# Shared remainder tiles in the last group of a graph-attention kernel, with a reordered lead-in and split borders

## The chip, the cores and the metric

One core of a Trainium2 chip runs the whole program. The metric is device time in microseconds (us). Five engines work side by side: TensorE (PE, with its weight loads as PEld), VectorE (DVE), ScalarE (ACT), GpSimd (POOL) and SyncE (SP, which here only issues DMAs). The kernel before takes 1327.33 us, the median of 3 runs from 1325.82 to 1328.85.

## The reference

A graph of 6250 nodes with 96 features and 106250 edges (50000 random ones in both directions, and a loop at every node). Each edge has a row node (`src`) and a column node (`dst`).

```python
q = (x[src] @ qW).reshape(e, 4, 24)
k = (x[dst] @ kW).reshape(e, 4, 24)
v = (x[dst] @ vW).reshape(e, 4, 24)
exp_s = exp(clip(einsum('ehd,ehd->eh', q, k), -10, 10))
norms = segment_sum(exp_s, src)[src]
w = exp_s / (norms + 1e-8)
res = segment_sum(w[:, :, None] * v, src).reshape(6250, 96)
y = x + (x + res)
out = (y - mean(y)) / sqrt(var(y) + 1e-5)      # over the 96 features
```

## The kernel before

The 6250 nodes are 49 blocks of 128. The kernel projects all nodes once: q stays in SBUF (`qt`), k and v go to a table in DRAM (`kv_table`, 192 numbers a row). The edges must be ordered by the block of their row node, because then one tile of 128 edges belongs to one block and a 128x128 one-hot matrix spreads q to the edges and adds the results up. The order is computed on the chip.

**Groups and sort.** The 106250 edges are cut into six groups of 140, 110, 130, 160, 160 and 150 columns of 125 edges. For each group a ranking stage (mostly DVE: `mark`, `tally`, `pair`, `pay`, `count`, `base`, `bounds`, `select`, `table`, `tree`, `own`) finds the place of each edge. Then come sort units (`unit`), one for 10 columns: DVE makes `lhs_1`, `lhs_a` and `lhs_b` (in the memory of `place_m`), ACT makes ten rows of `theta` (in `steps_m`), and PE adds 20 matmuls up in `ps_a` and `ps_b`. A border ends the group: `lower` (ACT copies the sums to `cum_a`, `cum_b`), `differ` (DVE: `dif`), `turn` (PE transposes, ACT copies to `turned`), `choice` (PE picks the tiles) and `pick` (DVE makes `dst_s`, the table rows to gather, and `loc_s`, the place in the block). Pieces of the sort of the next group stand between the batches of the one before.

**Tiles and batches.** A group gives tiles of 128 edges: 85, 110, 125, 155, 155 and 250, in all 880, worked on in 176 batches of five (U = 5). In groups 1 to 5 of the six only full tiles of a block are given out; what a block has left goes to the next group. The last group rounds every block up, so each block may end in a tile that is only partly filled: 250 tiles for 25610 edges (200 full tiles' worth).

**A batch.** POOL issues five indirect DMAs (line 474), each fetching 128 rows of `kv_table` into a slot of `kv`, a ring of R = 8 slots of five tiles. The wait before a batch's first gather is on `s_wv` (batch n-8 was weighed, so its slot is free) and on `s_res` (the results of batch n-6 are made, Y = 6). DVE builds `ohb`, PE transposes it to `ps_t`, ACT copies it to `onehT`, PE spreads q (`ps_q`, line 608), DVE multiplies by k (`prod`, line 1065), reduces and clips, ACT takes the exponential, DVE weighs v (`wv`, line 1074), PE sums (`ps_r`, line 622), DVE adds up in `acc` (line 1047). DVE waits for the gather at line 1065.

**What sets the order.** `plan()` writes a list of pieces and batches once, and each engine follows it, leaving out what it has no part in. In the lead-in the list places `lift` (transposes of x, `copy_xt`) and `project(i)` (seven blocks each) between pieces of the first ranking; `project(i)` of PE and ACT begins with the `lift` of i+1. `plan_last` runs the batches after the last border, 122 to 175, first some straight and then in a loop of eight. The end (`total`, `spread_of`, `root`, `scale_of`) divides, adds 2x and normalizes in four parts.

## Time and profile before

| | |
|---|---|
| median of 3 runs | 1327.33 us |
| profiled execution | 1328.32 us, span 1326.5 us |
| PE busy | 1016.5 us (77%) |
| DVE busy | 1027.9 us (77%) |
| ACT busy | 662.4 us (50%) |
| POOL busy | 935.0 us (70%) |
| gathers | 880, 86.56 MB |
| first gather starts | 97.67 us |
| last gather ends | 1286.34 us |
| mean granted PE clock | 0.716 of 2.4 GHz |

Busy time of an engine leaves out its issuing work. Of POOL above all: between two gathers of a batch the trace shows 0.30 us in which POOL waits for nothing that it shows. So an engine that is 70% busy can be one that never rests. The share says nothing of the stage either: the last stage, 971.5 to 1286.3 us, holds only batches and no sort.

### The profile page before, as it was taken

How to read it: one execution, taken by the hardware profiler on the slowest of the kernel's cores; microseconds unless marked ns; L12 is line 12 of the kernel's file. 1: busy time of each engine (PE TensorE's matmuls, PEld its weight loads, DVE VectorE, ACT ScalarE, POOL GpSimd, SP SyncE). 2: the span in 40 equal slices, each digit the busy share in tenths (PEclk: the TensorE clock that was granted, in tenths of full speed). 3: DMA queues.
4: the chain of work that ended last, by engine and by line, in shares of the span. 5: the costliest groups of instructions: out<-in, count | busy, mean ns of one | idle time of the engine just before them, and what ended most of it. 6: DMA issues, size and time to landing. Idle time of an engine off the chain costs nothing.

```text
span 1326.5 us, 23177 instructions
## 1 busy us (share of the span) xinstructions
PE 1016.5 (77%) x6512; PEld 920.2 (69%) x6513; DVE 1027.9 (77%) x3029; ACT 662.4 (50%) x1469; POOL 935.0 (70%) x912
## 2 busy tenths in 40 slices
PE   7876777688866888767878867877778888888870
PEld 5765776577756787657877656867677777777760
DVE  8889997899799998899977789877655555555557
ACT  5752692269622898224987322878332222222224
POOL 1207777777776777777777777777777777777762
PEclk9996698568975899765989666789765555555555
DMA  6202222222222222222222222222622222222222
GB/s 164 84 0 75 72 67 80 76 67 69 76 78 63 64 73 72 72 73 69 73 69 73 74 78 73 70 72 69 147 80 79 77 79 78 77 80 78 78 65 73
DMA packets 68434, 100.71 MB, mean 76 GB/s; under 512 B 33527, under 2 KB 54004, under 8 KB 68334
## 3 DMA queue, kind: packets, MB, share of 16 engines
q0 software_dynamic: 42240, 86.56, 24.0%
q1 hardware_dynamic: 26094, 12.94, 3.7%
q8 instruction: 47, 0.77, 0.2%
q14 instruction: 53, 0.43, 0.1%
HBM read 92.23 MB, written 7.22 MB: 75 GB/s over the span
## 4 chain that ended last, share of the span: by engine, by line
POOL 29%; DVE 25%; issue 17%; ACT 12%; PE 12%; DVEq 3%; DMA 2%; POOLq 0%; SPq 0%; ACTq 0%
POOL kv L474 28%; ACT steps_m L681 8%; DVE acc L1047 4%; PE ps_r L622 3%; DVE prod L1065 2%; PE ps_q L608 2%; ACT oneh L732 2%; DVE steps_m L806 2%; DMA kv<-kv_table,dst_s 2%; DVE place_m L948 2%; DVEq L391 2%; DVE place_m L952 2%; PE ps_a L594 2%; PE ps_b L594 1%; ACT onehT L726 1%
## 5 line engine op out<-in xcount | busy, mean ns | idle before, releaser
L474 POOL DMA_INDIRECT kv<-kv_table,dst_s x880 | 913.5, 1038 | 319.4 <-issue 313.0
L622 PE MATMUL ps_r<-wv,oneh 128*128 128x100 f32 x1752 | 339.8, 363 | 101.0 <-DVE wv L1074 100.4
L608 PE MATMUL ps_q<-qt,onehT 128*128 x1760 | 332.5, 357 | 97.8 <-ACT onehT L726 90.8
L622 PEld LDWEIGHTS ps_r<-wv,oneh 128*128 128x128 f32 x1752 | 309.2, 269 | 122.1 <-DVE wv L1074 116.2
L608 PEld LDWEIGHTS ps_q<-qt,onehT 128*128 128x128 f32 x1760 | 303.5, 263 | 124.9 <-issue 124.5
L681 ACT ACTIVATE steps_m<-iota_f,pos_t 125x254 f16<-125x254 f32 (+4 forms) x794 | 311.2, 484 | 17.4 <-PE ps_b L594 10.6
L1047 DVE TENSOR_TENSOR acc<-acc,ps_r 128x100 f32 x876 | 222.4, 254 | 58.7 <-issue 24.6
L1065 DVE TENSOR_TENSOR prod<-ps_q,kv 128x480 f32<-128x480 f32 x176 | 115.3, 655 | 175.5 <-DMA kv<-kv_table,dst_s 164.7
L719 ACT ACTIVATE wv<-clipped 128x20 f32<-128x20 f32 x176 | 38.3, 218 | 393.8 <-DVE clipped L1092 393.6
L726 ACT ACTIVATE onehT<-ps_t 128x640 f32<-128x640 bf16 x176 | 123.6, 702 | 180.5 <-PE ps_t L634 168.9
L594 PE MATMUL ps_a<-steps_m,place_m 125*128 125x254 f16 (+4 forms) x794 | 185.2, 283 | 28.6 <-ACT steps_m L681 28.0
L594 PE MATMUL ps_b<-steps_m,place_m 125*128 125x254 f16 (+4 forms) x794 | 183.6, 280 | 0.0
L732 ACT ACTIVATE oneh<-ohb 128x640 f32<-128x640 bf16 x176 | 163.1, 927 | 1.3 <-PE ps_r L622 1.3
L594 PEld LDWEIGHTS ps_a<-steps_m,place_m 125*128 125x128 f16 x794 | 112.3, 141 | 35.2 <-issue 16.0
L1074 DVE TENSOR_TENSOR wv<-kv,wv 128x480 f32<-128x480 f32 x176 | 114.3, 649 | 3.2 <-issue 2.2
L634 PE MATMUL ps_t<-ident_bf,ohb 128*128 128x128 bf16 x880 | 107.0, 271 | 11.7 <-DVE ohb L1055 11.5
L594 PEld LDWEIGHTS ps_b<-steps_m,place_m 125*128 125x128 f16 x794 | 112.8, 142 | 3.3
L1084 DVE TENSOR_REDUCE score<-prod 128x20 f32<-128x480 f32 x176 | 113.7, 646 | 0.2
L634 PEld LDWEIGHTS ps_t<-ident_bf,ohb 128*128 128x128 bf16 x880 | 92.4, 141 | 18.8 <-DVE ohb L1055 17.2
L1055 DVE TENSOR_TENSOR ohb<-iota_t,loc_s 128x640 bf16<-128x640 bf16 x176 | 98.8, 561 | 0.0
L988 DVE TENSOR_TENSOR place_m<-iota_s,pos_p 125x1280 f16<-125x1280 f16 x85 | 69.6, 819 | 8.7 <-PE ps_b L594 8.7
L992 DVE TENSOR_TENSOR place_m<-place_m,pay_a 125x1280 f16<-125x1280 f16 x85 | 69.7, 820 | 1.6
(196 smaller groups left out, 670.1 us busy)
## 6 DMA issues: line engine op xcount, KB each, us to landing
kv<-kv_table,dst_s POOLq DMA_INDIRECT x880
kv_table<-kv SPq DMA_DIRECT2D x7, 672.0 KB, 3.7
acc<-in_x_dram SPq DMA_DIRECT2D x6, 336.0 KB, 8.2
steps_m<-in_x_dram SPq DMA_DIRECT2D x6, 336.0 KB, 6.2
out_dram<-kv SPq DMA_DIRECT2D x6, 336.0 KB
dst_i<-in_dst_dram SPq DMA_DIRECT2D x1, 415.0 KB
src_i<-in_src_dram SPq DMA_DIRECT2D x1, 346.7 KB
acc<-in_x_dram SPq DMA_DIRECT2D x1, 288.0 KB, 4.7
```

Source lines behind the costliest of these rows:

```text
L474: nc.gpsimd.indirect_dma_start(kv[:, nm, u, :], None, kv_dram, bass.IndirectOffsetOnAxis(ap=dst_s[:, n * U + u:n * U + u + 1], axis=0)).th ...
L594: mm = nc.tensor.matmul(ps[:, 0:w], lhs[:, vm, :, j], steps, start=first and j == 0, stop=last and j == SU - 1)
L608: last = nc.tensor.matmul(ps_q[nm % 2][:, u * D:(u + 1) * D], onehT[:, nm % 2, u * P:(u + 1) * P], qt[:, bass.ds(blks[u], 1), :].rearrange ...
L622: last = nc.tensor.matmul(to, oneh[:, nm % 2, u, :], wv[:, nm % 2, u, :], start=True, stop=True)
L634: last = nc.tensor.transpose(ps_t[nm % 2][:, u * P // 2:(u + 1) * P // 2].bitcast(bf16), ohb[:, nm % 4, :, u], ident_bf[:, :])
L681: last = nc.scalar.activation(theta[:, vm, j, 0:w], iota_f[0:EP, 0:w], ACT.Sign, scale=-1.0, bias=pos_t[:, bass.ds(v * SU + j, 1)])
L726: nc.scalar.activation(onehT[:, nm % 2, :], ps_t[nm % 2][:, 0:U * P // 2].bitcast(bf16), ACT.Copy).then_inc(s_oneT, 1)
L732: nc.scalar.activation(oneh[:, nm % 2, :, :], ohb[:, nm % 4, :, :].rearrange("p n u -> p u n"), ACT.Copy).then_inc(s_onf, 1)
L1047: nc.vector.tensor_tensor(at, at, from_ps, ALU.add).then_inc(s_acc, 1)
L1065: nc.vector.tensor_tensor(prod[:, nm % 2, :].rearrange("p (u d) -> p u d", u=U), ps_q[nm % 2][:, 0:U * D].rearrange("p (u d) -> p u d", u= ...
L1074: nc.vector.tensor_tensor(wv[:, nm % 2, :, 0:D].rearrange("p u (h d) -> p u h d", h=HEADS), kv[:, nm, :, D:2 * D].rearrange("p u (h d) -> ...
L1084: nc.vector.tensor_reduce(score[:, nm % 2, :], prod[:, nm % 2, :].rearrange("p (h d) -> p h d", d=DH), axis=AX.X, op=ALU.add).then_inc(s_s ...
```

## The change

1. **Shared remainder tiles** (last group). The 250 tiles are now laid out as 25 pairs of blocks, 50 tiles that stand first, and 200 tiles of whole ones. A pair of blocks shares one gathered tile: the rest of the even block fills it from partition 0 on, that of the odd block from partition 127 down, since the position within a block is flipped for odd blocks (`flip`, an XOR with 127). Where two rests together exceed 128 edges, the odd block gets its own whole tile count instead. Each tile of the pair still has its own block, one-hot and batch, but both read the same slot of `kv`: batches 126 to 135 read the gathered batches 126 to 130, batches 136 to 175 the gathered 131 to 170 (`gathered`, `last_use`). POOL issues 171 batches of five and not 176. DVE, PE and ACT still work through 176.
2. **Gathers of the last group** wait on `s_wv` alone; the earlier ones keep the wait on `s_res`. `plan_last` runs batches straight up to 136 before its loop.
3. **Lead-in.** `project` no longer begins with a `lift`; the plan places both kinds.
4. **Sort units and borders.** PE does the ten matmuls of `ps_a`, then the ten of `ps_b`; the first ten wait for `lhs_a` alone. `lower`, `differ`, `turn` and `pick` signal and wait for each half. `pick` on DVE takes half a first.
5. **Small ones.** Two DVE instructions make `flip` in each group, `bounds` and `pick` of the last group get some more, and the last square root on ACT stands after 9 and not after 12 activations.

```diff
+    PAIRS = -(-NB // 2)
+    MT = 2 * PAIRS
+    GT.append(MT + alone)
...
+    def gathered(n):
+        if not isinstance(n, int) or n >= MB + MT // U:
+            return n - PAIRS // U
+        return n if n < MB else MB + (n - MB) // 2
+
+    def last_use(k):
+        if k < MB:
+            return k
+        return MB + 2 * (k - MB) + 1 if k < MB + PAIRS // U else k + PAIRS // U
...
-        looped = max(m, R)
+        looped = max(m, MB + MT // U + 1)
...
-        project_after = {"mark3": ("lift", 0), f"tally{len(ROUNDS[0]) - 1}": (1,), "base1": (2,),
-                         "table": (3, 4, 5, 6)}
+        between = {"mark3": (("lift", 0), ("lift", 1), ("project", 0)),
+                   f"tally{len(ROUNDS[0]) - 1}": (("lift", 2),), "count": (("project", 1),),
+                   "bounds": (("lift", 3), ("project", 2), ("lift", 4), ("project", 3)),
+                   "table": (("lift", 5), ("project", 4), ("lift", 6), ("project", 5), ("project", 6))}
...
-                for n in range(B0[g], B0[g + 1]):
+                for n in range(B0[g], B0[g + 1] if g < G - 1 else NG):
                     nm = n % R
-                    wait(pool, s_wv, n - R + 1)
-                    wait(pool, s_res, n - Y + 1)
+                    if n >= R:
+                        pool.wait_ge(s_wv, last_use(n - R) + 1)
+                    if Y <= n < MB:
+                        pool.wait_ge(s_res, last_use(n - Y) + 1)
...
-                pe.wait_ge(s_lhs, v + 1)
                 pe.wait_ge(s_theta, v + 1)
-                for j in range(SU):
-                    for ps, lhs in ((ps_a, lhs_a), (ps_b, lhs_b)):
+                for ps, lhs, s_made in ((ps_a, lhs_a, s_lhs_a), (ps_b, lhs_b, s_lhs)):
+                    pe.wait_ge(s_made, v + 1)
+                    for j in range(SU):
...
+                    if last and ps is ps_a:
+                        mm.then_inc(s_half, 1)
...
-                act.wait_ge(s_bin, V0[g + 1])
+                act.wait_ge(s_half, g + 1)
                 wait(act, s_sorted, g)
                 nc.scalar.activation(cum_a[:, 0:w], ps_a[:, 0:w], ACT.Copy).then_inc(s_cum, 1)
+                act.wait_ge(s_bin, V0[g + 1])
...
-                        if j + 1 < len(PARTS) and i == b - 1 and k == PC - 2:
+                        if j + 1 < len(PARTS) and i == b - 1 and k == (PC - 2 if b < NPC - 2 else 2):
...
+                    link(nc.vector.tensor_scalar(flip[:, 0:C], s, 7, 1, ALU.logical_shift_right, ALU.bitwise_and))
+                    link(nc.vector.tensor_scalar(flip[:, 0:C], flip[:, 0:C], float(P - 1), None, ALU.mult))
...
-                link(nc.vector.tensor_scalar(s, t, P - 1, None, ALU.bitwise_and))
+                link(nc.vector.scalar_tensor_tensor(s, t, P - 1, flip[:, 0:C], ALU.bitwise_and, ALU.bitwise_xor))
...
-                dve.wait_ge(s_pick, g + 1)
-                nc.vector.tensor_copy(b, ps_b[:, 0:T])
+                dve.wait_ge(s_pick, 2 * g + 1)
                 link(nc.vector.tensor_copy(a, ps_a[:, 0:T]))
-                link(nc.vector.tensor_scalar(b, b, 1, None, ALU.logical_shift_right))
...
+                dve.wait_ge(s_pick, 2 * g + 2)
+                link(nc.vector.tensor_scalar(b, ps_b[:, 0:T], 0.5, None, ALU.mult))
                 link(nc.vector.tensor_tensor(a, a, b, ALU.bitwise_or))
...
-                        dve.wait_ge(s_kv[nm], (n - nm) * (16 * U // R) + 16 * U)
+                        k, km = gathered(n), (gathered(n) if isinstance(n, int) else nm - PAIRS // U) % R
+                        dve.wait_ge(s_kv[km], (k - km) * (16 * U // R) + 16 * U)
```

How the first `count` moves on PE, in the lead-in, before and after. `ident_h` on `steps_m` is the tally, `ident_f` on `acc` a lift (the transposes of x), `w_all` a projection, `cnt` the count.

```order
L528 MATMUL ps_b<-steps_m,ident_h 125x196 x10
L500 MATMUL ps_q<-ident_f,acc 96x128 x7
L513 MATMUL ps_t<-w_all,acc 128x288
L513 MATMUL ps_r<-w_all,acc 128x288 x2
L513 MATMUL ps_t<-w_all,acc 128x288 x2
L513 MATMUL ps_r<-w_all,acc 128x288 x2
L535 MATMUL ps_a<-cnt,tri_h 128x49
L536 MATMUL ps_a<-cnt,ones_h 128x49
L500 MATMUL ps_q<-ident_f,acc 96x128 x7
```

```order
L551 MATMUL ps_b<-steps_m,ident_h 125x196 x10
L525 MATMUL ps_q<-ident_f,acc 96x128 x7
L558 MATMUL ps_a<-cnt,tri_h 128x49
L559 MATMUL ps_a<-cnt,ones_h 128x49
L536 MATMUL ps_t<-w_all,acc 128x288
L536 MATMUL ps_r<-w_all,acc 128x288 x2
L536 MATMUL ps_t<-w_all,acc 128x288 x2
L536 MATMUL ps_r<-w_all,acc 128x288 x2
L525 MATMUL ps_q<-ident_f,acc 96x128 x7
```

The count stood behind the second projection and now stands ahead of it. Farther down, the matmuls of `table`, which stood behind three projections (0, 1, 2), now stand behind four (0 to 3).

The first sort units on PE, before and after (`place_m` is `lhs`, `onehT` and `steps_m` are `theta`):

```order
L594 MATMUL ps_b<-onehT,place_m 128x186
L594 MATMUL ps_a<-onehT,place_m 128x186
L594 MATMUL ps_b<-onehT,place_m 128x186
L594 MATMUL ps_a<-steps_m,place_m 128x186
L594 MATMUL ps_b<-steps_m,place_m 128x186
L594 MATMUL ps_a<-steps_m,place_m 128x186
```

```order
L620 MATMUL ps_a<-onehT,place_m 128x186 x4
L620 MATMUL ps_a<-steps_m,place_m 128x186 x6
L620 MATMUL ps_b<-onehT,place_m 128x186 x4
L620 MATMUL ps_b<-steps_m,place_m 128x186 x6
L620 MATMUL ps_a<-onehT,place_m 128x186 x4
```

The two halves alternated and now follow each other; the number of matmuls is the same.

The end of the last border on DVE (`pick` of the last group), before and after (`cum_a` is the memory of the padding's rows):

```order
L1014 CAST bits_b<-ps_b 128x250
L1015 CAST bits_a<-ps_a 128x250
L1016 TENSOR_SCALAR bits_b<-bits_b 128x250
L1018 TENSOR_SCALAR iota_i<-bits_a 128x250
L1019 TENSOR_SCALAR cum_a<-iota_i,part_f 128x250
L1020 CAST loc_s<-iota_i 128x250
L1021 TENSOR_SCALAR bits_a<-bits_a 128x250
L1022 TENSOR_TENSOR bits_a<-bits_a,bits_b 128x250
L1023 TENSOR_TENSOR dst_s<-bits_a,cum_a 128x250
```

```order
L1063 CAST bits_a<-ps_a 128x250
L1065 TENSOR_SCALAR iota_i<-bits_a 128x250
L1066 TENSOR_SCALAR cum_a<-iota_i,part_f 128x250
L1067 CAST loc_s<-iota_i 128x250
L1068 TENSOR_SCALAR bits_a<-bits_a 128x250
L1070 TENSOR_SCALAR bits_b<-ps_b 128x250
L1071 TENSOR_TENSOR bits_a<-bits_a,bits_b 128x250
L1074 TENSOR_TENSOR cum_a<-cum_a 128x5x5
L1075 TENSOR_TENSOR bits_a<-bits_a 128x5x5
L1076 TENSOR_TENSOR dst_s<-bits_a,cum_a 128x25
L1079 TENSOR_TENSOR dst_s<-bits_a,cum_a 128x200
```

`dst_s` goes from 250 columns to 25 shared ones and 200; in every border the work on half a stands ahead of that on half b.

## Rows read from the trace of the kernel before

**Rows 1.** Page, chain that ended last by engine, and the gathers' group:
```profile
POOL 29%; DVE 25%; issue 17%; ACT 12%; PE 12%; DVEq 3%; DMA 2%; POOLq 0%; SPq 0%; ACTq 0%
...
L474 POOL DMA_INDIRECT kv<-kv_table,dst_s x880 | 913.5, 1038 | 319.4 <-issue 313.0
```
**Rows 2.** Groups by line, POOL, 97.6 to 971.4 us: busy, mean ns, idle:
```profile
L474 POOL DMA_INDIRECT kv<-kv_table,dst_s x630 | 674.6, 1071 | 243.3 <-issue 236.9 <-DVE wv L1074 3.7 <-PE ps_r L622 2.7
```
**Rows 3.** Groups by line, 971.4 to 1286.5 us, the last group's batches:
```profile
L474 POOL DMA_INDIRECT kv<-kv_table,dst_s x250 | 239.0, 956 | 76.2 <-issue 76.2
...
L1065 DVE TENSOR_TENSOR prod<-ps_q,kv 128x480 f32<-128x480 f32 x50 | 32.9, 658 | 117.7 <-DMA kv<-kv_table,dst_s 117.7
...
L1055 DVE TENSOR_TENSOR ohb<-iota_t,loc_s 128x640 bf16<-128x640 bf16 x49 | 27.3, 557 | 0.0
```
**Rows 4.** Stretches, line 474: stretch, length, POOL busy (x), PEclk, DMA, GB/s:
```profile
830.00:950.00 120.00, 93.97 (x86) 0.87 0.33 86
971.40:1286.50 315.10, 238.98 (x250) 0.52 0.29 78
```
**Rows 5.** Timeline, PE, around the last group's start: start, us, what, [idle]:
```profile
962.85 2.45 PE L608 MATMUL ps_q<-qt,onehT 128*128 x10 [0.88 <-ACT onehT L726]
...
968.85 2.45 PE L608 MATMUL ps_q<-qt,onehT 128*128 x10 [0.88 <-ACT onehT L726]
...
974.21 1.35 PE L608 MATMUL ps_q<-qt,onehT 128*128 x10 [0.88 <-ACT onehT L726]
...
977.84 1.35 PE L608 MATMUL ps_q<-qt,onehT 128*128 x10 [0.88 <-ACT onehT L726]
```
**Rows 6.** Timeline, DVE, first batch of the last group (number 126):
```profile
979.13 0.66 DVE L1065 TENSOR_TENSOR prod<-ps_q,kv 128x480 f32<-128x480 f32 x1 [2.22 <-DMA kv<-kv_table,dst_s]
```
**Rows 7.** Timeline, POOL, first and last of five waits over 0.30 us:
```profile
282.69 0.95 POOL L474 DMA_INDIRECT kv<-kv_table,dst_s  x1 [2.47 <-issue]
...
431.15 0.94 POOL L474 DMA_INDIRECT kv<-kv_table,dst_s  x1 [1.10 <-issue]
```
**Rows 8.** Timeline, all engines, lead-in to the first sort units:
```profile
17.57 0.19 DVE L845 CAST cnt<-cnt_f 125x49 f16<-125x49 f32 x1
...
20.44 0.21 DVE L853 TENSOR_SCALAR need_i<-ps_a 128x49 int32<-128x49 f32 x1 [2.68 <-PE ps_a L536]
...
30.61 1.13 ACT L656 ACTIVATE acc<-ps_q 96x512 f32<-96x512 f32 x2 [5.57 <-PE ps_q L500]
...
42.92 0.23 DVE L971 TENSOR_SCALAR pos_t<-tmp_i 125x140 f32<-125x140 int32 x1
...
47.73 0.41 ACT L668 ACTIVATE kv<-ps_r 128x288 f32<-128x288 f32 x1
48.04 4.18 ACT L681 ACTIVATE steps_m<-iota_f,pos_t 125x186 f16<-125x186 f32 x12
...
53.87 0.55 DVE L984 TENSOR_TENSOR onehT<-oneh,pos_h 125x744 f16<-125x744 f16 x1 [3.94 <-PE ps_b L594]
```
**Rows 9.** Timeline, all engines, last sort unit and border of the first group:
```profile
87.48 0.82 DVE L994 TENSOR_TENSOR place_m<-place_m,pay_b 125x1280 f16<-125x1280 f16 x1
...
88.36 0.36 PE L594 MATMUL ps_a<-onehT,place_m 125*128 125x186 f16 x1 [0.26 <-DVE place_m L994]
...
90.64 0.24 PE L594 MATMUL ps_b<-steps_m,place_m 125*128 125x186 f16 x1
...
91.14 0.32 ACT L703 ACTIVATE cum_b<-ps_b 128x186 f32<-128x186 f32 x1
...
94.67 0.25 DVE L1014 CAST bits_b<-ps_b 128x85 int32<-128x85 f32 x1 [2.70 <-PE ps_b L579]
...
96.40 0.25 DVE L1023 TENSOR_TENSOR dst_s<-bits_a,cum_a 128x85 int32<-128x85 int32 x1
...
97.67 1.22 POOL L474 DMA_INDIRECT kv<-kv_table,dst_s  x1 [44.28 <-issue]
```
**Rows 10.** Timeline, DVE, the end: its wait for the last root:
```profile
1318.77 0.24 DVE L1176 RECIPROCAL inv<-std 128x14 f32<-128x14 f32 x1 [1.53 <-ACT std L747]
```

More of the change, by code:

```diff
@@ L43, in gnn @@
         else:
-            GT.append(-(-((held + PAD) // P) // U) * U)
+            alone = -(-(held // P) // U) * U
+    PAIRS = -(-NB // 2)
+    assert PAIRS % U == 0
+    MT = 2 * PAIRS
+    GT.append(MT + alone)
     XC = PAD // P + U
@@ L61, in gnn @@
     NT, NBT = T0[G], B0[G]
+    NG = NBT - PAIRS // U
+    MB = B0[G - 1]
     CMAX, TMAX = max(GC), max(TS)
@@ L222, in gnn @@
         spread_f = cum_a
-        dst_s = sb("dst_s", [P, NT], i32)
+        flip = sb("flip", [EP, CMAX], i32)
+        dst_s = sb("dst_s", [P, NG * U], i32)
         loc_s = sb("loc_s", [P, NT], bf16)
@@ L539, in table @@
             def table(g):
-                w = GW[g]
+                w = GW[g] if g < G - 1 else alone
                 pe.wait_ge(s_after, g + 1)
@@ L575, in pick @@
                     if g:
-                        last = nc.tensor.matmul(ps[:, 0:XC], ident_h[:, :], over[:, i, :], start=False, stop=True)
+                        at = 0 if g < G - 1 else MT
+                        last = nc.tensor.matmul(ps[:, at:at + XC], ident_h[:, :], over[:, i, :], start=False, stop=True)
                     if g < G - 1:
@@ L896, in bounds @@
                 nc.vector.tensor_scalar(after[:, :], iota_f[0:NB, :], end_p[0:NB, 0:1], None, ALU.is_ge)
-                nc.vector.tensor_scalar(wafter[:, 0:GW[g]], iota_f[0:NB, 0:GW[g]], upto, None,
+                w = GW[g] if g < G - 1 else alone
+                nc.vector.tensor_scalar(wafter[:, 0:w], iota_f[0:NB, 0:w], upto, None,
                                         ALU.is_ge).then_inc(s_after, 1)
@@ L1071, in weigh @@
                     if there(n):
+                        km = (gathered(n) if isinstance(n, int) else nm - PAIRS // U) % R
                         dve.wait_ge(s_exp, n + 1)
```

95 lines of the change are left out of this document (58 added, 37 removed).

## The prediction

> **What bounds the kernel now.** I read the chain of waits first. The reader is to see that no engine has more than 29% of it, that POOL's share is nearly all line 474, and that 17% is "issue" [rows 1]. For POOL "issue" is not rest: the gathers' group has 319.4 us of idle time, of which 313.0 us is "issue" in front of 880 gathers, 0.36 us each. So I read POOL's groups by stretch. From 97.6 to 971.4 us it spends 674.6 + 243.3 us on 630 gathers, 1.457 us each; of the idle time only 3.7 + 2.7 us are waits for other engines [rows 2]. Five gathers start more than 0.30 us after the one before, all between 282.69 and 431.15 us, with 7.4 us of true waiting in all [rows 7]. In the last stretch there is none: 239.0 + 76.2 us for 250 gathers is 1.261 us each, 6.30 us a batch, and all 117.7 us for which DVE waits at line 1065 end with a gather's landing [rows 3]. From the first gather at 97.67 us [rows 9] to the end of the last, POOL is one unbroken row of gathers with 7.4 us of holes. The time is therefore: when POOL starts, plus the number of gathers times their pace, plus the holes, plus the tail behind the last one.
>
> **The sum.** It is made against the profiled execution (1328.3 us), which lies 1.0 us above the median of 1327.3.
>
> *Five batches less.* 25 gathers go, at the last group's pace [rows 3]: 25 x 1.261 = 31.5 us. This holds if the engines behind POOL keep up, since they still have 50 batches. Their own pace is on PE: from the start of one ps_q group to the next with no wait for a gather between it is 968.85 - 962.85 = 6.00 us at 1.2 GHz, and 977.84 - 974.21 = 3.63 us at 2.4 GHz [rows 5]. The first gathered batch serves two, so the first ten batches take 5 x 6.30 = 31.5 us of POOL and 60.0 us of PE at 1.2 GHz, 36.3 us at 2.4 GHz. PE falls 28.5 or 4.8 us behind. The 40 batches after them give back 0.30 us each at the lower clock and 2.67 us at the higher. To clear 28.5 us I need 7 of the 40 at 2.4 GHz (7 x 2.67 + 33 x 0.30 = 28.6). Now the clock stands at 0.52 there [rows 4], but PE waits for a gather in each batch; where it did not, from 962.85 to 974.21 us, the clock rose to the higher level within two batches [rows 5], and it is there that batch 126 begins [rows 6]. So I take all 31.5 us; the lower end is 28.5 - 40 x 0.30 = 16.5 us less, that is 15.0 us.
> The Trainium skill (TensorE: Matmul & The Clock Gate, Part 1) says that the gate grants the full rate to a PE that has been busy of late and half of it to one that has not; by that rule the catching up runs at the higher level, as the rise at 974.21 us agrees with, and the term is 31.5 us and not 15.0.
>
> *The ring.* POOL must not be stopped by the lag. Gather batch 12 of the group needs the slot of gather batch 4, which is free when batch 9 is weighed, at the lower clock some 62 us after the group's first gather has landed; its turn comes at 11 x 6.30 = 69 us. From there it needs batch j-3 for gather j, with a margin near 8 us. With the wait on s_res, two slots sooner, gather 10 would have stood about 9 us, so dropping that wait is what keeps the term whole. Cost 0.
>
> *Lead-in.* DVE had the counts ready at 17.76 us and got the sums at 20.44 [rows 8]; the count matmuls now stand ahead of the second projection, so DVE goes on at about 18.1 us, 2.3 us sooner, and pos_t is ready near 40.8 us and not 43.15. That alone does not start the sort: ACT finished the projections' copies at 48.1 us, and theta waited for that. ACT had 5.57 us idle ahead of 30.61 us, because PE held the next projections behind table. They now stand ahead; against that the second projection starts 1.3 us later, behind the count. ACT ends 4.3 us sooner, and about 1 us more since PE does not come out of a 5 us rest. So theta begins near 43 us, and DVE's third unit, which waited for PE's first one until 53.87 us [rows 8], comes 5.0 us sooner. The ends are 2.3 us (ACT gains nothing but DVE's part) and 7.3 us (the 3.94 us of DVE's wait go with the 2.3 and one more). The two flip instructions, 0.23 us each like their neighbours, lie ahead of the tally, where DVE waits for ACT anyway: 0.
>
> *First border,* which no batch covers. PE's last unit runs from 88.36 to 90.88 us [rows 9]. With lhs_a ready 0.82 us, one DVE instruction, before lhs_b, its first ten matmuls go ahead: -0.8 us. Then cum_b need not stand behind cum_a (-0.3), half b of turn and pick runs while half a is already in the next engine (-0.9), and five of DVE's instructions between 94.67 and 96.65 us are done before half b is there (-0.9). In all -2.9 us; ends -1 and -3.5.
>
> *Holes.* Consumers between 208 and 431 us decide the 7.4 us of holes. Two borders there get about 1.2 us shorter each, three groups' flips cost 0.5 us each: -0.9 us, with ends of -4 and +3.
>
> *The rest.* PE's new order has as many matmuls. The extra DVE instructions of the last group (some 3 us) fall where DVE is behind POOL's landing anyway and POOL has nothing to wait for: 0. The last root comes 3 activations (1.1 us) sooner and ends most of DVE's wait of 1.53 us, [rows 10], but the ACT work moved behind it holds the last stores about as long: -0.3 us, ends 0 and -1.0. While PE catches up, DVE is denser and gathers may stretch: +0.5 us.
> The ends of that last term come from rows: in 830 to 950 us, beside the sort, a gather takes 93.97 / 86 = 1.093 us, in the last stretch 0.956 us [rows 4]. If the 135 gathers of a long catching up took the former, it would be 135 x 0.137 = +18.5 us; I stay near zero because the 49 ohb instructions (0.557 us each) and all other batch work lie beside the 250 gathers already [rows 3].
> The Trainium skill (SBUF — State Buffer, "SBUF: two separate sides") speaks against the change here: a DVE instruction in a two-port mode locks GpSimd out, so the DMA's descriptors are not written until it ends. If every ohb were such a lock, 49 x 0.557 = 27 us would already sit in the last stretch; the mean of 0.956 us against gathers of 0.94 [rows 7] leaves room for about 4 us.
>
> Sum: -31.5 - 5.0 - 2.9 - 0.9 - 0.3 + 0.5 = -40.1, so 1288.2 us in a profiled execution and 1287.2 us as median. I forecast 1287.
>
> **The rivals.**
> - *PE stays at 1.2 GHz and never catches up.* Then PE's 6.00 us sets the last group and the term is 15.0 us: 1287.2 + 16.5 = 1304. For it: the mean clock of 0.52 [rows 4]. Against: the rise described.
> - *The front gives nothing at the end.* An earlier start is only worth what the holes do not take back; if lead-in and border gains become longer holes before 431 us: 1327.3 - 31.5 = 1296. Against: the consumers start sooner by the same amount.
> - *Gathers stretch while DVE is dense:* up to 18.5 us, 1306. Against: the mean in rows 3.
> - *The pairs bring nothing,* because a batch of a pair waits as long as before (the change does not do what it says): 1327.3 - 8.6 = 1319.
> - *Slower: the sort units lose the clock.* PE now waits for theta before anything else and does its twenty matmuls in two rows on one bank each. A unit of the first group took 90.88 - 88.36 = 2.52 us [rows 9] for 186 columns, so 3.4 us for 254; at half the clock it could cost up to 3.4 us more. With 71 units in the later groups (710 columns) it decides from 40 / 3.4 = 12 units on, and at 20 units the time is 1287 + 68 = 1355. Against: the count of matmuls is the same, and PE is granted 0.87 in that stretch [rows 4].
>
> **How the numbers follow.** Forecast 0.76; PE too slow 0.09; front without gain 0.07; stretched gathers 0.03; pairs without gain 0.02; slower 0.03. The forecast's own range, from the ends of the small terms, is 1281 to 1293. The front's case at 1296 belongs in the range and a part of PE's, half caught up: 1280 to 1298 leaves out 0.17. Faster than before by over 0.2% (2.7 us, about what a measurement of this kernel can tell from no change): all but the last case, 0.96; same 0.01; slower 0.03.
>
> **What would show it.** 855 gathers and not 880; the first near 90 us; theta's first near 43 us; the end of the last gather near 1246 us; DVE's wait for gathers gone in batches 127 to 136 and back before 160; a clock well over 0.52 in the first 60 us of the last group; no wait of POOL longer than 0.3 us there; gathers still at 0.95 to 0.97 us. The forecast is wrong if the last stage's batches run at 6.0 us to the end, if POOL's holes grow, or if the first gather starts after 93 us.

## The result, and the profile after

| | before | after |
|---|---|---|
| median | 1327.34 us (4 runs, 1325.82 to 1328.85) | 1288.15 us (4 runs, 1285.94 to 1290.72) |
| profiled execution, span | 1328.32, 1326.5 us | 1285.94, 1284.1 us |
| first gather starts | 97.67 us | 89.44 us |
| first gather of the last group | 971.51 us | 959.48 us |
| last gather ends | 1286.34 us | 1243.83 us |
| mean granted clock | 0.716 | 0.734 |

The ratio is 0.9705, interval 0.9683 to 0.9728: 39.2 us less. The forecast was 1287. On another chip the same kernel came to 1285.9 us against 1327.74, ratio 0.9677 (0.9658 to 0.9695).

The page after, the chain by engine and the groups that answer to [rows 1] and to DVE's waits for gathers:

```profile
POOL 27%; DVE 25%; issue 15%; ACT 14%; PE 12%; DVEq 3%; DMA 2%; SPq 0%; POOLq 0%; ACTq 0%
...
L499 POOL DMA_INDIRECT kv<-kv_table,dst_s x855 | 890.0, 1041 | 305.3 <-issue 298.9
...
L1122 DVE TENSOR_TENSOR prod<-ps_q,kv 128x480 f32<-128x480 f32 x176 | 115.0, 653 | 144.1 <-DMA kv<-kv_table,dst_s 138.5
```

25 gathers are gone and POOL is still first in the chain, two points lower. Over the whole kernel DVE waited 164.7 us for gathers before and waits 138.5 us now.

Groups by line for POOL, 89.4 to 959.45 us, as in [rows 2]:

```profile
L499 POOL DMA_INDIRECT kv<-kv_table,dst_s x630 | 673.9, 1070 | 236.8 <-issue 231.0 <-DVE wv L1132 4.9 <-PE ps_r L650 0.9
```

and 959.45 to 1244 us, as in [rows 3]:

```profile
L499 POOL DMA_INDIRECT kv<-kv_table,dst_s x225 | 216.1, 960 | 68.5 <-issue 67.9 <-DVE wv L1132 0.6
...
L1122 DVE TENSOR_TENSOR prod<-ps_q,kv 128x480 f32<-128x480 f32 x50 | 32.8, 656 | 88.7 <-DMA kv<-kv_table,dst_s 88.6
```

The last group's gathers take (216.1 + 68.5) / 225 = 1.265 us each, against 1.261 before. DVE's waits for them fell from 117.7 to 88.6 us, and these 29.1 us are nearly the whole gain of the last group.

The same last group in stretches, line 499 (stretch, its length, POOL busy, PEclk, DMA share, GB/s), as in [rows 4]:

```profile
830.00:950.00 120.00, 93.80 (x87) 0.84 0.35 92
959.45:1020.00 60.55, 46.20 (x48) 0.94 0.29 79
1020.00:1244.00 224.00, 169.90 (x178) 0.52 0.28 78
```

The clock stands at 0.94 for 60 us and then at the old 0.52. The border between the two is near the batch at which DVE waits for gathers again. DVE's timeline, batches 126, 127, 135, 136, 139 and 140 (start, us, what, [idle before it]), which answers to [rows 6]:

```profile
967.39 0.66 DVE L1122 TENSOR_TENSOR prod<-ps_q,kv 128x480 f32<-128x480 f32 x1 [2.67 <-DMA kv<-kv_table,dst_s]
970.95 0.65 DVE L1122 TENSOR_TENSOR prod<-ps_q,kv 128x480 f32<-128x480 f32 x1
...
1001.03 0.65 DVE L1122 TENSOR_TENSOR prod<-ps_q,kv 128x480 f32<-128x480 f32 x1
1004.85 0.65 DVE L1122 TENSOR_TENSOR prod<-ps_q,kv 128x480 f32<-128x480 f32 x1
...
1018.07 0.66 DVE L1122 TENSOR_TENSOR prod<-ps_q,kv 128x480 f32<-128x480 f32 x1 [1.39 <-DMA kv<-kv_table,dst_s]
1024.36 0.66 DVE L1122 TENSOR_TENSOR prod<-ps_q,kv 128x480 f32<-128x480 f32 x1 [2.04 <-DMA kv<-kv_table,dst_s]
```

Batch 126 waits for its gather, batches 127 to 138 do not, batch 139 (1018.07 us) does again, and from there a batch takes 6.3 us. PE's ps_q groups in between, as in [rows 5]:

```profile
972.17 1.35 PE L636 MATMUL ps_q<-qt,onehT 128*128 x10 [0.94 <-ACT onehT L752]
975.86 1.35 PE L636 MATMUL ps_q<-qt,onehT 128*128 x10 [0.94 <-ACT onehT L752]
```

They follow each other in 3.69 us, at the high level of the clock. All engines in the catching up and behind it (stretch, its length, then PE, PEld, DVE, ACT and POOL busy, PEclk, DMA share, GB/s):

```profile
970.00:1005.00 35.00, 26.01 (x239) 24.51 (x238) 30.87 (x95) 16.28 (x29) 26.60 (x28) 1.00 0.30 80
1020.00:1244.00 224.00, 187.04 (x883) 170.34 (x881) 121.88 (x356) 61.57 (x107) 169.90 (x178) 0.52 0.28 78
```

While batches are caught up DVE is the fullest engine, busy 30.87 of 35.00 us. From 970.95 to 978.60 us, two batches, its only pauses are two of 0.19 and 0.18 us, while PE rests 0.94 us ahead of each ps_q group.

POOL's waits over 0.30 us, the first and the last of four, as in [rows 7], and DVE's wait for the last root, as in [rows 10]:

```profile
274.92 0.94 POOL L499 DMA_INDIRECT kv<-kv_table,dst_s  x1 [2.48 <-issue]
...
428.60 0.94 POOL L499 DMA_INDIRECT kv<-kv_table,dst_s  x1 [1.08 <-issue]
```

```profile
1275.30 0.24 DVE L1234 RECIPROCAL inv<-std 128x14 f32<-128x14 f32 x1 [0.45 <-ACT std L773]
```

A hole is such a wait of POOL, counted beyond the 0.30 us that stand between any two gathers. 4.2 us of holes are left of 7.4, and none of them is in the last group.

The lead-in and the first border, all engines, with the rows that answer to [rows 8, 9]:

```profile
18.61 0.21 DVE L881 TENSOR_SCALAR need_i<-ps_a 128x49 int32<-128x49 f32 x1 [0.32 <-PE ps_a L559]
...
31.27 0.97 ACT L684 ACTIVATE acc<-ps_q 96x512 f32<-96x512 f32 x2 [0.41 <-PE ps_q L525]
...
41.37 0.23 DVE L1020 TENSOR_SCALAR pos_t<-tmp_i 125x140 f32<-125x140 int32 x1
...
42.55 0.41 ACT L694 ACTIVATE kv<-ps_r 128x288 f32<-128x288 f32 x1
42.86 4.19 ACT L707 ACTIVATE steps_m<-iota_f,pos_t 125x186 f16<-125x186 f32 x12
...
82.25 0.82 DVE L1044 TENSOR_TENSOR place_m<-place_m,pay_b 125x1280 f16<-125x1280 f16 x1
...
89.44 1.23 POOL L499 DMA_INDIRECT kv<-kv_table,dst_s  x1 [40.92 <-issue]
```

DVE's wait for the count fell from 2.68 to 0.32 us, ACT's rest from 5.57 to 0.41 us. The last `lhs_b` of the first group begins at 82.25 us and not 87.48: 5.23 us for the lead-in. From there to the first gather it is 7.19 us and not 10.19: 3.00 us for the border.

The start of all this moves from trace to trace. In the eleven traces of kernels with the new lead-in, those of the experiments included, DVE's `need_i` behind the first count starts between 18.08 and 19.91 us. Distances counted from it are firmer: from `need_i` to the first gather it is 70.83 us here and 70.5 to 70.8 us in eight of the nine other traces with the new border too (72.59 in one). Before it was 77.23 us, of which 3.00 are the border's. So counted from `need_i` the lead-in gives 3.40 us, and 2.36 us are saved ahead of it in the wait for the count: 5.8 us, of which the start took 0.5 back in this pair of traces.

### The profile page after: what moved, and what is told of

The parts are those of the page before. It is cut to its first block, busy times and chain, and to the rows that moved or that the text cites. A ratio compares the mean times of both kernels' runs of the same rounds, so it can differ in the third digit from the quotient of the medians.

```text
span 1284.1 us, 23009 instructions
## 1 busy us (share of the span) xinstructions
PE 988.8 (77%) x6512; PEld 897.6 (70%) x6513; DVE 1030.2 (80%) x3048; ACT 660.6 (51%) x1469; POOL 912.9 (71%) x887
## 4 chain that ended last, share of the span: by engine, by line
POOL 27%; DVE 25%; issue 15%; ACT 14%; PE 12%; DVEq 3%; DMA 2%; SPq 0%; POOLq 0%; ACTq 0%
POOL kv L499 27%; ACT steps_m L707 10%; DVE acc L1103 5%; PE ps_r L650 3%; PE ps_q L636 2%; DVE prod L1122 2%; ACT oneh L758 2%; DMA kv<-kv_table,dst_s 2%; DVEq L414 2%; DVE place_m L997 2%; DVE steps_m L834 2%; DVE place_m L1001 2%; PE ps_a L620 1%; ACT onehT L752 1%; PE ps_b L620 1%
## 5 line engine op out<-in xcount | busy, mean ns | idle before, releaser
L499 POOL DMA_INDIRECT kv<-kv_table,dst_s x855 | 890.0, 1041 | 305.3 <-issue 298.9
L636 PE MATMUL ps_q<-qt,onehT 128*128 x1760 | 322.3, 348 | 103.7 <-ACT onehT L752 91.0
L650 PE MATMUL ps_r<-wv,oneh 128*128 128x100 f32 x1752 | 329.9, 356 | 91.7 <-DVE wv L1132 91.4
L636 PEld LDWEIGHTS ps_q<-qt,onehT 128*128 128x128 f32 x1760 | 293.0, 255 | 131.2 <-issue 130.7
L650 PEld LDWEIGHTS ps_r<-wv,oneh 128*128 128x128 f32 x1752 | 301.7, 263 | 109.5 <-DVE wv L1132 105.7
L1122 DVE TENSOR_TENSOR prod<-ps_q,kv 128x480 f32<-128x480 f32 x176 | 115.0, 653 | 144.1 <-DMA kv<-kv_table,dst_s 138.5
L620 PE MATMUL ps_a<-steps_m,place_m 125*128 125x254 f16 (+4 forms) x794 | 107.7, 287 | 26.8 <-ACT steps_m L707 26.8
L620 PEld LDWEIGHTS ps_a<-steps_m,place_m 125*128 125x128 f16 x794 | 88.0, 142 | 35.0 <-ACT steps_m L707 29.0
L662 PE MATMUL ps_t<-ident_bf,ohb 128*128 128x128 bf16 x880 | 103.9, 266 | 9.6 <-DVE ohb L1111 9.1
L620 PE MATMUL ps_b<-steps_m,place_m 125*128 125x254 f16 (+4 forms) x794 | 101.8, 277 | 0.0
L620 PEld LDWEIGHTS ps_b<-steps_m,place_m 125*128 125x128 f16 x794 | 89.7, 141 | 4.1
```

Of the source, the lines that this page charges most:

```text
L499: nc.gpsimd.indirect_dma_start(kv[:, nm, u, :], None, kv_dram, bass.IndirectOffsetOnAxis(ap=dst_s[:, n * U + u:n * U + u + 1], axis=0)).th ...
L620: mm = nc.tensor.matmul(ps[:, 0:w], lhs[:, vm, :, j], steps, start=first and j == 0, stop=last and j == SU - 1)
L636: last = nc.tensor.matmul(ps_q[nm % 2][:, u * D:(u + 1) * D], onehT[:, nm % 2, u * P:(u + 1) * P], qt[:, bass.ds(blks[u], 1), :].rearrange ...
L650: last = nc.tensor.matmul(to, oneh[:, nm % 2, u, :], wv[:, nm % 2, u, :], start=True, stop=True)
L662: last = nc.tensor.transpose(ps_t[nm % 2][:, u * P // 2:(u + 1) * P // 2].bitcast(bf16), ohb[:, nm % 4, :, u], ident_bf[:, :])
L1122: nc.vector.tensor_tensor(prod[:, nm % 2, :].rearrange("p (u d) -> p u d", u=U), ps_q[nm % 2][:, 0:U * D].rearrange("p (u d) -> p u d", u= ...
```

## The experiments

Each kernel is the changed one with the edit shown. The first four (old lead-in, old border, no shared tiles, wait kept) ran on one chip, where the kernel before took 1327.25 us (11 runs). The wait kept and the changed kernel ran again on a second such chip (1327.74 us). The six from "Three of five gathers left out" on ran on two other chips, which gave longer times for every kernel, the one before included: 1554.43 us (gathers left out, batches made slower, ring alone) and 1536.21 us (ring alone again, count alone). Only ratios to it, and stretches free of the cause, are used from them; the last section deals with that.

### The old order of the lead-in

```diff
-                   f"tally{len(ROUNDS[0]) - 1}": (("lift", 2),), "count": (("project", 1),),
-                   "bounds": (("lift", 3), ("project", 2), ("lift", 4), ("project", 3)),
-                   "table": (("lift", 5), ("project", 4), ("lift", 6), ("project", 5), ("project", 6))}
+                   f"tally{len(ROUNDS[0]) - 1}": (("lift", 2), ("project", 1)),
+                   "base1": (("lift", 3), ("project", 2)),
+                   "table": (("lift", 4), ("project", 3), ("lift", 5), ("project", 4), ("lift", 6), ("project", 5),
+                             ("project", 6))}
```

> The changed kernel with the lead-in in its old order (count behind the second projection, table ahead of the fourth). Theory (POOL's row of gathers sets the time, an earlier first gather is worth itself): first gather near 94.5 us and not 89.4, all later gathers shifted by the same, time 1288 + 5 = 1293 us. Rival (the front's gain is taken back by POOL's holes before 431 us): first gather later too, but the last gather ends where it did, 1288 us.

Measured: 1294.72 us, ratio 0.9739 (0.9713 to 0.9764), 4.5 us above the first result's ratio. DVE waits 2.69 us for the count again, and ACT's first theta comes at 49.70 us. POOL, the first gather and the last one:

```profile
95.99 1.22 POOL L500 DMA_INDIRECT kv<-kv_table,dst_s  x1 [40.74 <-issue]
...
1251.19 0.95 POOL L500 DMA_INDIRECT kv<-kv_table,dst_s  x1 [0.30 <-issue]
```

The first gather starts 6.55 us later than in the changed kernel and the last one ends 8.31 us later. From the first gather to batch 126 it is 871.8 us, inside the 868.0 to 873.8 us of all traces from these chips, so the later start is not taken back on the way; the rival's 1288 us falls. Of the 6.55 us, 0.8 are no cost of the edit: `need_i` starts at 21.75 us here, 1.3 us later than in the kernel before with the same order, and DVE is that much later before its wait for the count begins, a shift that kernels with one and the same lead-in show too. Counted from `need_i` the first gather comes 74.24 us later, and 77.23 - 3.00 = 74.23 in the kernel before: the lead-in is worth 5.8 us.

### The old border

```diff
-                for ps, lhs, s_made in ((ps_a, lhs_a, s_lhs_a), (ps_b, lhs_b, s_lhs)):
-                    pe.wait_ge(s_made, v + 1)
-                    for j in range(SU):
+                pe.wait_ge(s_lhs, v + 1)
+                for j in range(SU):
+                    for ps, lhs in ((ps_a, lhs_a), (ps_b, lhs_b)):
...
-                act.wait_ge(s_half, g + 1)
+                act.wait_ge(s_bin, V0[g + 1])
```

`turn` and `pick` signal once for both halves again too.

> The changed kernel with sort units and borders as before (ps_a and ps_b alternate, one signal for both halves in lower, differ, turn and pick). Theory: first gather 2.9 us later, near 92.3 us; the later borders act only through POOL's holes, which were 4.2 us in the changed kernel and 7.4 before, so up to 3 us more; time 1291 to 1294 us. Rival (a border is worth something only where it is uncovered): 2.9 us at the first and nothing after, 1291 us with holes of 4 us.

Measured: 1291.54 us, ratio 0.9735 (0.9709 to 0.9761), 4.0 us above the first result's. The last unit and the border, DVE and POOL:

```profile
81.77 0.82 DVE L1039 TENSOR_TENSOR place_m<-place_m,pay_b 125x1280 f16<-125x1280 f16 x1
...
88.95 0.25 DVE L1059 CAST bits_b<-ps_b 128x85 int32<-128x85 f32 x1 [2.70 <-PE ps_b L603]
...
91.96 1.22 POOL L499 DMA_INDIRECT kv<-kv_table,dst_s  x1 [43.97 <-issue]
```

From `lhs_b` to the gather it is 10.19 us, to the hundredth what it was before, and DVE waits 2.70 us for `pick` as in [rows 9]. So the border's 3.00 us are point 4 of the change. The edit takes back the order of the matmuls, the signals for each half and the order in `pick` together, so it doesn't tell them apart. The later borders can't be read from it: holes grew to 6.8 us, but from the first gather to batch 126 it is 872.2 us, inside the range above, and 1291.54 fits the theory and its rival alike.

### No shared tiles

```diff
-            alone = -(-(held // P) // U) * U
-    PAIRS = -(-NB // 2)
+            alone = -(-((held + PAD) // P) // U) * U
+    PAIRS = 0
```

With it `flip` is held at 0, and the pairs' instructions in `bounds` and `pick` go.

> The changed kernel with 880 gathers again: the last group has 250 tiles with a gather each, the rest of the change stays. Theory: +25 x 1.25 us = +31 us, 1319 us, with the first gather still at 89.4 us and POOL without a hole in the last group. Rival (the faster front gave more than it seems and the sharing less): clearly under 1315 us.

Measured: 1315.33 us, ratio 0.9923 (0.9899 to 0.9947). The last group's gathers:

```profile
L499 POOL DMA_INDIRECT kv<-kv_table,dst_s x250 | 239.7, 959 | 76.1 <-issue 76.1
```

The last group takes 315.6 us and not 284.4: the sharing is worth 31.2 us, and all the rest of the change 1327.25 - 1315.33 = 11.9 us (7.0 to 13.4 by the interval). By the ratios the sharing is worth (0.9923 - 0.9705) x 1327 = 29 us. The time lies between the theory's 1319 us and what the rival asked for (clearly under 1315); the last group's own 31.2 us bear the theory out, and this trace has the shortest way from the first gather to batch 126 of all, 868.0 us.

### The wait on the results kept in the last group

```diff
-                    if Y <= n < MB:
+                    if Y <= n:
```

> The changed kernel with the wait on s_res kept in the last group too. Theory from the trace after (PE catches up at 2.4 GHz, 3.8 us a batch, so results of batch n-6 are ready before its gather's turn): no change, 1288 us, no hole in the last group. Rival (the prediction's sum at 1.2 GHz, gather 10 of the group stands 9 us): a hole of several us near 1016 us and up to 1297 us.

> The changed kernel with the wait on s_res kept in the last group. On a chip where the kernel before takes 1327 us: the same as the changed kernel within 3 us. On a chip where it takes 1536 us or more: theory, faster than the changed kernel by the longer pauses of the last group, 10 to 30 us; rival (the pauses have nothing to do with how far POOL is ahead), the same.

Measured: 1285.44 us, ratio 0.9685 (0.9658 to 0.9712), and on another chip, beside the changed kernel there, 1288.64 us, 0.9684 (0.9652 to 0.9716). No difference from the changed kernel (0.9705 and 0.9677). POOL in the last group (first of the two traces, 963.0 to 1246.8 us):

```profile
L499 POOL DMA_INDIRECT kv<-kv_table,dst_s x225 | 215.5, 958 | 68.5 <-issue 67.9 <-DVE wv L1132 0.6
```

It is the changed kernel's row but for 0.6 us, and no wait on `ps_r` is in it. Dropping `s_res` there is worth nothing. The prediction's 9 us stand of gather 10 does not exist.

> The changed kernel itself, once more, next to the one below on one chip. If the chip is like that of the first comparison (the kernel before takes 1327 us): 1288 us. If it is like the two chips on which the kernel before took 1536 to 1554 us: theory (there the engines pause until POOL's gathers stop, so gathers farther ahead make the pauses longer, and the last group has lost the wait that held POOL back) no faster than before; rival (25 gathers less are 31 us on any chip): 2% faster than before on that chip too.

The changed kernel again, on the same chip as the second of these: 1285.9 us (1283.8 to 1290.86), last group 285.1 us. Its profiled execution has the first gather at 90.34 us and the last end at 1248.16 us, 4.3 us later than the first trace. One trace of one kernel is good to about that; terms of a few us are believed only where rows show them on the spot, as in the lead-in and border.

### Three of five gathers left out

In the last group only two of a batch's five gathers are issued, so that POOL cannot be what sets its pace. The other k and v rows aren't fetched, and those tiles work on stale ones.

```diff
+                        if n >= MB and u > 1:
+                            continue
```

> Leaves out three of the five gathers of every batch of the last group (those tiles work on stale rows), so POOL needs 2.5 us a batch and cannot set the pace. It measures what the engines behind POOL need by themselves. Theory: PE runs without waits, the clock goes to 2.4 GHz and stays there, 3.8 us a batch as in batches 127 to 137 of the changed kernel, the last group takes about 190 us and not 284, time near 1195 us. Rival (the prediction's lower end: PE stays at 1.2 GHz and 6.0 us a batch): 300 us, time near 1300 us.

Measured, in one run: 1375.85 us, on the chip where the kernel before takes 1554.43. The last group takes 196.3 us for 50 batches, 3.93 us each, at a granted clock of 0.92 (one of the stops of the last section, 6 us, lies in it). POOL in it (stretch, its length, POOL busy, PEclk, DMA share, GB/s):

```profile
1112.90:1309.10 196.20, 86.51 (x90) 0.92 0.19 50
```

PE's ps_q groups in the middle of it:

```profile
1161.28 1.35 PE L638 MATMUL ps_q<-qt,onehT 128*128 x10 [1.15 <-ACT onehT L754]
1164.97 1.35 PE L638 MATMUL ps_q<-qt,onehT 128*128 x10 [0.94 <-ACT onehT L754]
1168.66 1.35 PE L638 MATMUL ps_q<-qt,onehT 128*128 x10 [0.94 <-ACT onehT L754]
```

3.69 us from one to the next, as in [rows 5] at the high clock and as in the changed kernel's first twelve batches. PE rests about 1 us ahead of each group here too (0.88 to 1.50 us in the last 18 of them), and the clock stays high. So the low clock of the last group is a result of the gathers' pace and no property of the stage's work: with three of five gathers gone it is 0.92 over 196 us.

### Batches made slower

Four more reductions of `prod` on DVE in each batch of the last group, with the shared tiles and without.

```diff
+                        for extra in range(4 if not isinstance(n, int) or n >= MB else 0):
+                            nc.vector.tensor_reduce(spare[:, nm % 2, extra, :],
+                                                    prod[:, nm % 2, :].rearrange("p (h d) -> p h d", d=DH),
+                                                    axis=AX.X, op=ALU.add)
```

> The changed kernel with four more reductions on DVE in each batch of the last group (results thrown away), 4 x 0.57 us, which makes DVE's own pace about 6.0 us a batch and so the engines behind POOL about as slow as PE at 1.2 GHz would be. Theory (sharing is worth its 25 gathers only while the rest can catch up): first product at 967 us, then 49 x 6.0, the last near 1261 us and not 1247, time 1302 us. Rival (DVE has 38% idle time in the last stage, so 2.3 us a batch are free): 1288 us.

> The kernel with 880 gathers and the rest of the change, with the same four reductions more in each batch of the last group. Theory: 6.0 us a batch is below POOL's 6.3 us, nothing has to be caught up, so no change, 1315 us; the same addition that costs 14 us with shared tiles costs 0 here. Rival (DVE is on the path of the batches at any rate): 1315 + 14 us or more.

Measured: 1584.22 and 1606.55 us, ratios 1.012 (1.0051 to 1.019) and 1.0276 (1.0195 to 1.0358), last groups 397.8 and 402.7 us. Both are above the kernel before, and of the two the one with shared tiles is the shorter, 22 us where the theory had 13 and the rival 41 or more. For the question asked this is inconclusive: on that chip the engines stand still many times. Waits in the last group with shared tiles (engine, line, for what: us in total, times, longest):

```profile
ACT onehT L753 <- remote: 149.8, 18, 29.5
POOL kv L500 <- DVE wv L1133: 110.2, 24, 10.5
...
DVE acc L1104 <- remote: 59.4, 11, 13.6
```

What sharing is worth when DVE is the slower side can't be read from lengths that hold 150 us of such waits.

### The ring alone everywhere

```diff
-                    if Y <= n < MB:
-                        pool.wait_ge(s_res, last_use(n - Y) + 1)
```

> The changed kernel with the wait on s_res taken out in all groups, so POOL waits for the ring of eight slots alone. Theory: up to about 431 us the consumers set the time and POOL's holes only mop up the difference (first gather to batch 49 took 339 to 342 us in every kernel so far, with holes of 0.8 to 7.4 us), so POOL gets at most some 2 us farther ahead before it waits for s_wv: 0 to -2 us, 1286 to 1288. Rival (the holes are lost time): all 2 to 4 us of holes go and the time falls by as much, 1284 us.

> The same kernel as e6_ring_all (no wait on s_res in any group), again, because the chip of that call ran every kernel some 17% longer, the kernel before too (1554 us). Theory: the order of that call is a trait of the chip, where gathers far ahead came with pauses of all engines but POOL; on a chip where the kernel before takes 1327 us, 1286 to 1288 us. Rival (gathering farther ahead is what costs, on any chip): clearly over 1300 us.

Measured: 1706.26 us, ratio 1.0933 (1.088 to 1.0986), and on the second of these chips 1662.98 us, 1.0827 (1.0778 to 1.0876). Next to the count-only kernel (below), 1544.52 us on the second of these chips, it is 8% more. What those chips do while POOL is not stopped has a large part in it (last section). On a chip of 1327 us this wasn't tried, so whether the ring alone costs anything there is open, and with it the theory and the first rival.

### Only the count moved

`project` 2 and 3 go back to where they stood, the count stays ahead of the second projection.

```diff
-                   "bounds": (("lift", 3), ("project", 2), ("lift", 4), ("project", 3)),
-                   "table": (("lift", 5), ("project", 4), ("lift", 6), ("project", 5), ("project", 6))}
+                   "base1": (("lift", 3), ("project", 2)),
+                   "table": (("lift", 4), ("project", 3), ("lift", 5), ("project", 4), ("lift", 6), ("project", 5),
+                             ("project", 6))}
```

> The changed kernel with the count ahead of the second projection, but table ahead of the fourth as before. Theory (the first sort units wait for ACT's projections, which end 4 to 5 us sooner only through the move of table): first gather near 94 us, so most of the 6.5 us that the old order costs remain, time 1292 us. Rival (DVE's 2.3 us of sooner pos_t are what counts): first gather near 90 to 92 us, 1289 us.

Measured: 1544.52 us, ratio 1.0047 (1.0009 to 1.0085) to the kernel before on that chip. The lead-in has no waits of the kind above, so its rows can be read (DVE, ACT, POOL):

```profile
18.45 0.21 DVE L882 TENSOR_SCALAR need_i<-ps_a 128x49 int32<-128x49 f32 x1 [0.32 <-PE ps_a L560]
...
43.39 4.19 ACT L708 ACTIVATE steps_m<-iota_f,pos_t 125x186 f16<-125x186 f32 x12
...
89.97 1.23 POOL L500 DMA_INDIRECT kv<-kv_table,dst_s  x1 [41.53 <-issue]
```

Theta starts at 43.39 us against 42.86, the first gather at 89.97 against 89.44. Counted from `need_i` it is 71.52 us to the first gather, 70.83 in the changed kernel and 74.23 in the old order: the count's move brings about 5.1 of the 5.8 us, the projections ahead of table some 0.7, on one trace.

How it does that stands in the rows of the first matmul of table on PE, in the kernel before and here, and in ACT's rest behind it here (5.57 us before, [rows 8]):

```profile
29.18 0.29 PE L543 MATMUL ps_a<-wafter,weigh_h 49*128 49x138 f16 x1 [4.58 <-DVE wafter L897]
```

```profile
26.71 0.23 PE L567 MATMUL ps_a<-wafter,weigh_h 49*128 49x138 f16 x1 [0.63 <-DVE wafter L930]
...
27.63 0.97 ACT L685 ACTIVATE acc<-ps_q 96x512 f32<-96x512 f32 x2 [1.10 <-PE ps_q L526]
```

PE stood 4.58 us ahead of table for `wafter`, which DVE makes from the count, and ACT's rest hung on that. With the count alone moved DVE starts `wafter` 2.5 us sooner and PE ends the second projection 1.5 us later, so PE stands 0.63 us and ACT 1.10.

## Why the prediction was right, point by point

| term | predicted | measured |
|---|---|---|
| 25 gathers fewer, with the stretch | -31.5 + 0.5 | 314.83 to 284.35 us: -30.5 |
| lead-in | -5.0 | -5.23 |
| first border | -2.9 | -3.00 |
| first gather to batch 126 (holes) | -0.9 | 873.84 to 870.04 us: -3.8 |
| behind the last gather | -0.3 | 40.16 to 40.27 us: +0.1 |
| profiled spans | -40.1 | 1326.5 to 1284.1: -42.4 |

The medians differ by 39.2 us. The first three terms came out nearly as predicted. The -3.8 us of the fourth are no measure of it: that way takes 868.0 to 873.8 us in eight traces, 870.0 and 872.8 in two of the changed kernel itself, and why it differs was not found. So the 2.3 us by which the profiled gain exceeds the sum are within what two traces of one kernel differ by.

*Five batches less.* Right, with its mechanism. Batches 126 to 136 took 1004.85 - 967.39 = 37.5 us where 36.3 was said, so the engines were 37.5 - 31.5 = 6.0 us behind and not 4.8, and then gained 6.3 - 3.8 = 2.5 us a batch until batch 139. With three of five gathers left out the clock is 0.92 over the whole group, so the high level goes with batches that don't wait for gathers. The Trainium skill (TensorE: Matmul & The Clock Gate, Part 1) gives the full rate to a PE that has been busy of late and half of it to one that has not. The trace agrees with it only in part: the clock is high where batches follow without a wait and low where they wait, but by busy time PE is the busier at the low level, 187.04 of 224.00 us at 0.52 against 26.01 of 35.00 at 1.00. The text gave the pace of the catching up to PE; at the high level it is rather DVE's, which has hardly a pause in these batches while PE rests 0.94 us in each. The pace it took, 3.63 us from PE's rows, came close to the measured 3.75 all the same. The rival in which PE stays at 1.2 GHz fell at once; what it would cost was never seen, because no run held PE low during the catching up.

*The ring.* Here the working was wrong, though it cost nothing. It took the margin from the lag at 1.2 GHz ("at the lower clock some 62 us") in the same text that let PE run at 2.4 GHz for the sum, and so "dropping that wait is what keeps the term whole". With a lag of 6 us and not 28.5, POOL has no hole in the last group even where the wait on `s_res` is kept. Putting it back changed nothing on two chips.

*Lead-in.* The size and the start of theta (43 us, measured 42.86) are right, and so is what theta waits for, ACT's last projection copy, which starts at 42.55 us. The division is wrong. The text gave the count 2.3 us and the rest to projections that now stand ahead of table. The run with the count alone shows the opposite: with the projections back behind the table matmuls the first gather comes only 0.5 to 0.7 us later. What the text left out is that table on PE waits for what DVE makes from the count, so an earlier count also releases the projections behind table earlier. The size held all the same, because it was taken from ACT's rest of 5.57 us, which goes either way.

*First border.* Right: 3.00 us, seen both in the change and, in reverse, in the run with the old border. Of its four terms only the first was looked at by itself: PE's last unit starts 0.23 us behind the start of `lhs_b` (82.48 and 82.25) and not 0.88, which is -0.65 where -0.8 was said.

*Holes.* The sum said POOL is one unbroken row with 7.4 us of holes, so that a hole less is time less. The traces disagree for the first half. From the first gather to batch 49 it is 340.81 us before with 7.36 us of holes, 339.16 after with 4.23, 339.42 without sharing with 0.80, 340.39 with the old border with 6.83, and with the wait on the results kept 341.83 with 2.19. Holes differ by 6.6 us and the stretch by 2.7, and not in the same order: where a hole goes, the gathers themselves take longer (the 245 of them are busy 259.1 us before, 260.6 after and 264.2 without sharing). That would fit engines behind POOL that set this stretch, but why the gathers lengthen isn't shown; no experiment on a chip of 1327 us took the holes away. The rival "the front gives nothing at the end" fell: the stretch nearly kept its length and starts 8.23 us sooner. The reason given, that those engines start sooner by the same amount, agrees with that and wasn't tested by itself.

A figure in the first part is wrong as well. 674.6 + 243.3 us over 630 gathers holds the 44.28 us of idle time ahead of the first gather. Without them it is 1.387 us each, and 1.381 after. No term rested on the 1.457.

*The rest.* The last root's wait fell from 1.53 to 0.45 us [rows 10] and the end gained nothing, as the text half expected. The extra DVE instructions are not to be seen.

*Gathers beside a dense DVE.* 0.960 us against 0.956: 0.9 us over 225 gathers. The Trainium skill (SBUF — State Buffer, "SBUF: two separate sides") has GpSimd locked out while DVE is in a two-port mode. The first 60 us, with half as many DVE instructions again per us, give 46.20 / 48 = 0.963 us a gather against 169.90 / 178 = 0.954 behind them, so no such price shows here; which of these instructions, if any, is in such a mode no run tells.

*Slower: the sort units lose the clock.* Fell. PE is granted 0.84 in 830 to 950 us against 0.87, and a unit of the first group, at the full clock in both, takes 2.51 us (82.48 to 84.99) against 2.52. For the later groups, which the rival was about, the way from the first gather to batch 126 is the answer: 870.0 us against 873.8, where it asked for 40 us more at least.

## What to carry to other kernels

Ask of each stage which engine never rests, counting the issue time between its instructions and not its busy share, and take work off that one: 10% of the last group's gathers were worth 10% of the group, because the engines behind had a pace of 3.8 us against POOL's 6.3. A clock that reads low in such a stage may be a result of the waiting, so price the catching up at the pace that batches show where none waits. When a piece of work moves ahead, look for what else waits for its result: the count's move was worth 5 us and not 2.3 because table waited for it too. Subtract the two traces stage by stage from an event of each, since their starts can differ by over 1 us. And work out every part of a forecast at the same clock: a margin for waits taken at one level beside a sum taken at the other found a stall that was never there.

## What the runs showed of the hardware that was not expected

The kernel before took 1327 us in the first comparison and on two more chips, and 1554 and 1536 us on two others, 17 and 16% more. Those last two are the chips of the six experiments from the left-out gathers on. The durations of the work are the same there (the last group's gathers 0.960 us in the count-only run, DVE's prod 653 ns in both), and no trace of the chips of 1327 us holds a wait of the kind below. What is new are waits of ACT and DVE that the profile puts down to "remote", no queue that it knows: 315.9 us in 56 pieces at ACT's `onehT` alone in the count-only run. The chain of the run with the ring alone (second time) has them as its largest part:

```profile
another core or an unknown queue 27%; PE 24%; DVE 16%; ACT 15%; issue 14%; DVEq 2%; ACTq 0%; POOL 0%; POOLq 0%
```

PE, ACT and DVE stop together while POOL goes on gathering. The first long one, count-only run, all engines:

```profile
126.96 0.94 POOL L500 DMA_INDIRECT kv<-kv_table,dst_s  x1 [0.30 <-issue]
132.40 0.21 DVE L879 SCALAR_TENSOR_TENSOR need_i<-ps_a,rest 128x49 int32<-128x49 f32 x1 [21.74 <-remote]
132.42 0.70 ACT L753 ACTIVATE onehT<-ps_t 128x640 f32<-128x640 bf16 x1 [22.79 <-remote]
...
140.88 0.94 POOL L500 DMA_INDIRECT kv<-kv_table,dst_s  x1 [12.98 <-PE ps_r L651]
```

and the same place with the ring alone, on the same chip:

```profile
140.40 0.95 POOL L497 DMA_INDIRECT kv<-kv_table,dst_s  x1 [0.30 <-issue]
145.21 0.70 ACT L750 ACTIVATE onehT<-ps_t 128x640 f32<-128x640 bf16 x1 [32.56 <-remote]
...
147.27 0.21 DVE L876 SCALAR_TENSOR_TENSOR need_i<-ps_a,rest 128x49 int32<-128x49 f32 x1 [33.47 <-remote]
...
153.24 1.06 POOL L497 DMA_INDIRECT kv<-kv_table,dst_s  x1 [11.88 <-DVE wv L1130]
```

In both, the other engines come back 4 to 6 us after POOL's last gather has ended (127.90 and 141.35 us). With the wait on `s_res` POOL runs out after six batches, with the ring alone after eight, ten gathers of 1.25 us later, and the stop lasts 10 to 12 us longer. The other four kernels of these chips show the same: three with the wait on `s_res` come back at 132.6 to 133.3 us, 4.6 to 4.9 us after their thirtieth gather has ended, and the ring alone on the other chip at 146.8, 6.1 us after its fortieth. So at this place the stop lasts until the gathers run out, whatever the kernel, and a shallower lead of POOL ends it sooner; whether the 8 to 9% that it costs to take the wait away everywhere come from many such stops wasn't counted. What the engines wait for is not shown. Between 110.2 and 132.4 us the count-only trace has packets of the gathers' queue alone and none of an instruction queue, so no record speaks for an instruction load.

Two things stay open. The count-only kernel, which differs from the changed one by under 1 us in the lead-in, is at 1.0047 to the kernel before on such a chip, so the 3% of the change may not be had there; the changed kernel itself did not run on one. And whether the last group's missing wait on `s_res` is part of that, or the wait kept would bring the 3% back, wasn't tried. On the chips of 1327 us the kept wait costs nothing (0.9684 and 0.9685). No version was found that beats the changed kernel.
